# Keys turned by DVE and DMA instead of by PE in a lightning-attention and MoE layer

## The reference, cut to what matters

```python
qkv = jax.nn.silu(jnp.einsum('bnf,of->bno', x, w_qkv))
q, k, v = jnp.split(qkv, 3, axis=-1)
def step(kv, blk):
    qi, ki, vi = blk
    o_inter = jnp.einsum('bhmd,bhde->bhme', qi * q_decay, kv)
    qk = jnp.einsum('bhmd,bhnd->bhmn', qi, ki) * diag_decay
    o_intra = jnp.einsum('bhmn,bhne->bhme', qk, vi)
    kv_new = block_decay * kv + jnp.einsum('bhmd,bhme->bhde', ki * k_decay, vi)
    return (kv_new, o_inter + o_intra)
```

## Time and profile before

| | |
|---|---|
| time, median of 3 runs | 1790.89 us (1789.92 to 1792.35) |
| profiled execution | 1791.69 us, of which the profile's span is 1788.9 us |
| PE, DVE, ACT, POOL busy | 98%, 69%, 40%, 33% of the span |
| TensorE clock | granted 0.998 of full speed over the span |
| DMA | 249.37 MB, mean 139 GB/s |

### The profile page before, as it was taken

How to read it: one execution, slowest core, us unless ns; L and a number is a source line. 1 busy time by engine, 2 the same in 40 slices (tenths; PEclk the granted TensorE clock), 3 DMA queues, 4 the chain that set the end, 5 groups by cost and what they waited for, 6 DMA issues and landing times.

```text
span 1788.9 us, 34315 instructions
## 1 busy us (share of the span) xinstructions
PE 1751.8 (98%) x12213; PEld 1565.2 (87%) x12213; DVE 1228.4 (69%) x2463; ACT 709.8 (40%) x1331; POOL 585.8 (33%) x794
## 2 busy tenths in 40 slices
PE   6999999999999999999999999999999999999998
PEld 5888899999888888888888888889999999999997
DVE  7888777777566665666656666667777777766566
ACT  4333333343444444444444444443434343333332
POOL 2222254544434333433334333323232323200011
PEclk9999999999999999999999999999999999999999
DMA  6665431322367676676766766623222222210013
GB/s 216 220 222 210 139 110 62 108 86 83 106 196 225 199 220 204 205 215 201 215 210 203 218 201 207 210 71 95 63 83 71 72 72 71 74 46 1 1 60 106
DMA packets 194872, 249.37 MB, mean 139 GB/s; under 512 B 27280, under 2 KB 161936, under 8 KB 194704
## 3 DMA queue, kind: packets, MB, share of 16 engines
q1 hardware_dynamic: 150032, 138.09, 26.0%
q0 software_dynamic: 32256, 83.93, 14.4%
q10 hardware_dynamic: 12416, 25.17, 3.8%
HBM read 135.92 MB, written 111.17 MB: 138 GB/s over the span
## 4 chain that ended last, share of the span: by engine, by line
PE 93%; DVE 4%; issue 2%; ACT 1%; DMA 1%; SPq 0%; POOL 0%; DVEq 0%; ACTq 0%; POOLq 0%
PE bank L1166 7%; PE bank L1146 7%; PE bank L1168 7%; PE bank L1167 7%; PE bank L1148 7%; PE bank L1147 7%; PE bank L1190 6%; PE bank L1207 6%; PE bank L1198 6%; PE bank L1210 6%; PE bank L1230 5%; PE bank L1238 3%; PE bank L1219 3%; PE bank L1221 3%; PE bank L1220 3%; PE bank L1183 3%
## 5 line engine op out<-in xcount | busy, mean ns | idle before, releaser
L520 POOL DMA_DIRECT2D xsT<-rows_turned x384 | 209.9, 553 | 331.8 <-PE bank L1230 188.9
L1166 PE MATMUL bank<-wh,xh 128*128 128x256 f32 x1024 | 311.0, 304 | 0.0
L614 ACT ACTIVATE kv<-bank 128x512 f32<-128x512 f32 x256 | 152.9, 597 | 342.2 <-PE bank L1168 342.2
L1168 PE MATMUL bank<-wh,xl 128*128 128x256 f32 x1024 | 288.6, 282 | 0.0
L1167 PE MATMUL bank<-wl,xh 128*128 128x256 f32 x1024 | 288.2, 281 | 0.0
L529 POOL DMA_INDIRECT yk<-slot_y,pos x128 | 127.5, 996 | 278.1 <-DVE xr L930 229.8
L958 DVE SCALAR_TENSOR_TENSOR state<-state,hc,bank 128x128 f32<-128x128 f32 x448 | 155.8, 348 | 85.0 <-PE bank L1198 71.4
L1166 PEld LDWEIGHTS bank<-wh,xh 128*128 128x128 f32 x1024 | 193.8, 189 | 15.9 <-issue 15.9
L1146 PE MATMUL bank<-xh,wh 128*128 128x512 f32 x512 | 207.2, 405 | 0.0
L1148 PE MATMUL bank<-xh,wl 128*128 128x512 f32 x512 | 202.4, 395 | 0.0
L1147 PE MATMUL bank<-xl,wh 128*128 128x512 f32 x512 | 201.9, 394 | 0.0
(11 more groups left out here) (162 smaller groups left out, 3637.6 us busy)
## 6 DMA issues: line engine op xcount, KB each, us to landing
slot_x<-zeros ACTq DMA_DIRECT2D x8, 3072.0 KB, 9.9
we<-wexp_in SPq DMA_DIRECT2D x192, 128.0 KB, 2.4
xs<-slot_x SPq DMA_DIRECT2D x96, 256.0 KB, 3.7
rows_turned<-xz POOLq DMA_DIRECT2D x96, 256.0 KB, 2.8
xsT<-rows_turned POOLq DMA_DIRECT2D x384, 64.0 KB, 2.7
slot_y<-ys SPq DMA_DIRECT2D x96, 256.0 KB, 2.7
wd<-wdown_in SPq DMA_DIRECT2D x192, 64.0 KB, 2.5
raw<-wqkv_in SPq DMA_DIRECT2D x16, 384.0 KB, 4.0
```

The costliest lines, as they stand in the source:

```text
L520: pool.dma_start(xsT[q % 2][b * TB:(b + 1) * TB, :, :, :].rearrange("p a k j -> p a (k j)"), xz_back[q % 2, b]).then_inc(xsT_loaded[q % 2] ...
L614: act.activation(kv[i % 2][:, 2 * half:2 * half + 2, :].rearrange("p c n -> p (c n)"), bank[half][:], ACT.Silu).then_inc((k_silu, v_silu)[ ...
L1166: pe.matmul(dst, lh, rh, start=(k == 0), stop=False)
L1168: mm = pe.matmul(dst, ll, rh, start=False, stop=(k == KD - 1))
```

## The change

DVE turns the keys in blocks of 32x32 within their partitions, in one instruction (`kz`). SP stores them to DRAM (`keys_turned`), and after that has landed SP loads them in four DMAs, each of which moves the blocks of one group of 32 features to its partitions (`kT_by_group`). ACT then sets the blocks side by side (`kT`), one slot after the keys were made. PE's transposes and their bank use are gone; its scores move behind the first half of the output projection. DVE's `update_state` and `gated` move ahead of `decay_scores`. SP's program is written by slot, since it now has work in each: its older waits and DMAs are put to slots.

```diff
+            def store_keys(i):
+                sp.wait_ge(kz_ready, i + 1)
+                sp.dma_start(kz_dram[i % 2], kz[:].rearrange("p b c j -> p b (c j)")).then_inc(kz_stored, 16)
+
+            def load_keys(i):
+                sp.wait_ge(kz_stored, 16 * (i + 1))
+                sp.wait_ge(kT_ready, i)
+                for b in range(BLK):
+                    sp.dma_start(kT_by_group[b * TB:(b + 1) * TB, :, :, :].rearrange("p a c j -> p a (c j)"),
+                                 kz_back[i % 2, b]).then_inc(kT_loaded, 16)
...
+            for s in range(SLOTS + 1):
+                q0 = 2 * (s - EXPERT0)
+                experts = EXPERT0 <= s < EXPERT1
+                if EXPERT0 < s <= EXPERT1:
+                    pair_done(q0 - 1)
+                if s > FIRST_OUT + 3:
+                    store_last(s - FIRST_OUT - 4)
+                if s < NSTEP:
+                    store_keys(s)
+                if s in COMBINE:
+                    store_part(COMBINE.index(s))
+                if EXPERT0 - 1 <= s < EXPERT1:
+                    load_rows(q0 + 4)
+                if s < NSTEP:
+                    load_keys(s)
+                if 4 <= s < ROUTE0 + 3 * NSB and s % 3 == 1:
+                    load_rows_to_scatter(s // 3)
+                if s == EXPERT0 - 2:
+                    first_pairs()
+                if experts:
+                    pair_done(q0)
+                if EXPERT0 - 1 <= s < EXPERT1:
+                    load_rows(q0 + 5)
...
-            def copy_kT(i):
-                act.wait_ge(kT_mm, i + 1)
-                act.copy(kT[:], bank[2][:]).then_inc(kT_ready, 1)
+            def copy_kT(j):
+                act.wait_ge(kT_loaded, 16 * BLK * (j + 1))
+                act.wait_ge(s_mm, j)
+                act.copy(kT[:].rearrange("p c a j -> p a c j"), kT_by_group[:]).then_inc(kT_ready, 1)
...
+            def turn_keys(i):
+                dve.wait_ge(k_silu, i + 1)
+                dve.wait_ge(v_silu, i + 1)
+                dve.wait_ge(kz_stored, 16 * i)
+                dve.transpose(kz[:], kv[i % 2][:, :, 0:HD].rearrange("p c (b i) -> p b c i", i=TB)).then_inc(kz_ready, 1)
...
-            def turn_keys(i):
-                pe.wait_ge(sm_ready, i)
-                pe.wait_ge(mask_ready, NSB)
-                for c in range(CH):
-                    mm = pe.transpose(bank[2][:, ch[c]], kv[i % 2][:, c, 0:HD], ident[:])
-                mm.then_inc(kT_mm, 1)
```

More of the change, by code:

```diff
@@ L66, in lightning_moe @@
     xz_dram = nc.dram_tensor("rows_turned", [2, P, BLK, 4 * TB], F32, kind="Internal").ap()
+    kz_dram = nc.dram_tensor("keys_turned", [2, P, BLK, CH * TB], F32, kind="Internal").ap()
     part2 = nc.dram_tensor("part2", [T, D], F32, kind="Internal").ap()
@@ L252, in lightning_moe @@
         q_mm = sem("q_mm")
-        kT_mm = sem("kT_mm")
+        kz_ready = sem("kz_ready")
+        kz_stored = sem("kz_stored")
+        kT_loaded = sem("kT_loaded")
         g_mm = sem("g_mm")
@@ L385, in _, with load_rows_to_scatter @@
                 group(g)
[L387 to L391, removed]
+            def store_keys(i):
[7 more added lines that the diff above has]
+                                 kz_back[i % 2, b]).then_inc(kT_loaded, 16)
+            def load_rows_to_scatter(q):
                 for r in range(CH):
@@ L408, in load_experts, with first_pairs, pair_done @@
                     sp.dma_start(wd[r][j * F:(j + 1) * F, :], at(wdown, e)).then_inc(pair_loaded[r], 16)
[L410 to L429, removed]
+            def first_pairs():
+                sp.wait_ge(routed, 1)
+                sp.wait_ge(wgt_ready, 1)
+                for q in range(2):
+                    load_experts(q)
+                for r in range(CH):
+                    sp.wait_ge(scattered[r], 16 * TOPK * NT // CH)
+                for q in range(2):
+                    load_rows(q)
+            def pair_done(q):
+                sp.wait_ge(y_mm, q + 1)
+                if q + 2 < NPAIR:
+                    load_experts(q + 2)
+                sp.wait_ge(ys_ready, q + 1)
+                sp.dma_start(slot_y_pair[q], ys[q % 2][:]).then_inc(y_stored[q % 2], 16)
             def load_part(t):
@@ L433, in load_part, with store_part @@
                 sp.dma_start(xr[t % 2][:], part_tile[t]).then_inc(xr_loaded[t % 2], 16)
[L435 to L439, removed]
-                if s in COMBINE:
[L441 to L445, removed]
+            def store_part(t):
+                sp.wait_ge(summed, TOPK * (t + 1))
+                sp.dma_start(part2_tile[t], xr[t % 2][:]).then_inc(part2_stored[t % 2], 16)
@@ new lines, in load_last, with store_last @@
+            def load_last(b):
+                if b < 2:
+                    for r in range(2):
+                        sp.wait_ge(part2_stored[r], 16 * NT // 2)
+                else:
+                    sp.wait_ge(out_stored[b % 2], 16 * (b // 2))
+                sp.dma_start(res[b % 2][:], part2_grp[b]).then_inc(res_loaded[b % 2], 16)
+            def store_last(b):
+                sp.wait_ge(final, CH * (b + 1))
+                sp.dma_start(out_grp[b], res[b % 2][:]).then_inc(out_stored[b % 2], 16)
@@ new lines, in _ @@
+            sp.wait_ge(xn_stored, 16 * NSB)
+            next_head(1)
+            load_rows_to_scatter(0)
+            for s in range(SLOTS + 1):
[7 more added lines that the diff above has]
+                    store_keys(s)
+                if s in COMBINE:
+                    store_part(COMBINE.index(s))
[11 more added lines that the diff above has]
+                    load_rows(q0 + 5)
+                if s == EXPERT1:
+                    for r in range(2):
+                        sp.wait_ge(y_stored[r], 16 * NPAIR // 2)
+                    for t in range(2):
+                        load_part(t)
+                if s in COMBINE and COMBINE.index(s) + 2 < NT:
+                    load_part(COMBINE.index(s) + 2)
@@ L446, in _ @@
                 if s % NSB == 5 and s // NSB + 2 < NH:
                     next_head(s // NSB + 2)
[L449 to L458, removed]
+                if s == FIRST_OUT:
+                    for b in range(2):
+                        load_last(b)
@@ L1030, in _ @@
                     combine(COMBINE.index(s))
+                if s < 2:
+                    dve.wait_ge(tab_stored, 16)
+                if projects:
+                    turn_keys(s)
+                if attends:
+                    update_state(s - 1)
+                if experts:
+                    gated(q0)
                 if attends:
                     decay_scores(s - 1)
[L1033 to L1038, removed]
                 if projects:
@@ L1188, in scores @@
                 pe.wait_ge(kT_ready, j + 1)
+                pe.wait_ge(sm_ready, j)
+                pe.wait_ge(mask_ready, NSB)
                 for c in range(CH):
-                    mm = pe.matmul(bank[2][:, ch[c]], kT[:, ch[c]], qT[:, ch[c]], start=True, stop=True)
+                    mm = pe.matmul(bank[2][:, ch[c]], kT[:, c, :, :].rearrange("p a j -> p (a j)"), qT[:, ch[c]], start=True, stop=True)
                 mm.then_inc(s_mm, 1)
@@ L1276, in _ @@
                     project_kv(s, 0)
-                if attends:
-                    scores(s - 1)
+                    project_kv(s, 1)
                 if s > FIRST_OUT + 2:
                     turn_back(s - FIRST_OUT - 3)
[L1281 to L1284, removed]
                 if s == 0:
@@ L1290, in _ @@
                     keys_values(s - 1)
+                if experts:
+                    gate_up(q0)
                 if delivers:
                     project_out(s - 2, 0)
+                if attends:
+                    scores(s - 1)
                 if experts:
```

12 lines of the change are left out of this document (8 added, 4 removed).

## The result

The changed kernel takes 1848.9 us (median of 4, 1843.6 to 1852.1) against 1790.7: a ratio of 1.032, 95% interval 1.030 to 1.034. It is slower by 58 us, on the side that had 0.47, and outside my range of 1756 to 1820. The profiled execution, the fastest of the four, took 1843.6 us, its span 1841.8.

What follows compares the result with a forecast made beforehand. PE was taken to bound the kernel, with SP becoming the bound in expert slots: 1791.7 - 35.2 (PE) + 4 (DVE) + 6 (start) + 2 (slots 25, 26) + 20.2 (expert slots) = 1789 us, range 1756 to 1820.

Steps and rivals of the forecast that it cites:

- the side that had 0.47: Whole kernel: the chance given to the change making it slower, against 0.42 for faster and 0.11 for the same.
- PE's part: All 128 slots: dropping four transposes shortens PE by 0.44 us a slot, 0.11 each, 56 us in all.
- DVE's chain: Key turn, state steps and mask before PE's attend: fits with 0.15 us to spare; 4 us cost in all, 0 to 13.
- DVE did not become the bound: Rival: turn, state and mask late by 0.3 us each slot, PE waits before attend, 1809 us; chance 0.05.
- The start: Slot 1's scores: the first keys come late behind SP's row loads, so PE waits 6 us, 5 to 7.
- Slots 25 and 26: First experts' loads stand behind slot 25's key loads, and the key turn is queued behind: 2 us added, 0 to 6.
- The landing of the keys' store, in SP's round: Expert slots: SP waits for its store to land, taken as 3.0 us, before four loads; adds 20.2 us over 48 slots.
- 10.5 + 2.5 + 1.8 = 14.8 us: SP's round per expert slot: own work, landing less 0.5 us overlap, four issues; against 13.94 us for PE alone.
- the upper bound of the round: SP's round in expert slots: at most 16.2 us, with landing 3.7 and issues 2.5; lower bound 13.9.
- SP falls well behind: Rival, expert slots: landing 3.5, issues 0.5 and slowed transfers make SP's round 15.4 us, 1817 us; chance 0.18.
- SP keeps up: Rival, expert slots: landing 2.1 us, round 13.9, PE stays the bound and wins there too, 1747 us; chance 0.15.
- The Trainium skill's fit for a DMA: Keys' store landing: 2.0 us plus bytes at 436 GB/s, 2.6 us for 256 KB; round 14.4, end 1769 us.

Runs made afterwards that it cites:

- e4_store_first: The changed kernel with the keys' store issued ahead of the result store slot_y, not behind it; ratio 1.016 to the kernel before on the same chip.
- c_before: The kernel before, unchanged, run and traced again on a slow chip; 1889.5 us there, one run of 1890.9 us.
- e3_trip_alone: The kernel before, PE still turning the keys, plus DVE's turn and SP's store and loads that nobody reads; ratio 1.050 to the kernel before.
- e1_fill_wait: The changed kernel with the expert slots' four key loads issued after the slot's second pair is done; ratio 1.000 to the kernel before.

## Why the prediction was wrong

**PE's part held.** Without the transposes the step from the last gate matmul to the second of the next slot is 0.35 us, as said (timeline, PE, changed kernel; the earlier trace rows had 0.79):

```profile
1261.52 0.40 PE L1199 MATMUL bank<-xh,wl 128*128 128x512 f32 x1
1261.75 0.28 PE L1217 MATMUL bank<-wh,xh 128*128 128x256 f32 x1
1261.87 0.28 PE L1218 MATMUL bank<-wl,xh 128*128 128x256 f32 x1
```

Combining slots came to 10.55 (I had 10.5). As the earlier trace rows together say, the 0.27 us of a transpose's row is its length, and what its removal gives back is the distance of starts, 0.11.

**DVE's chain** had 4 us in my sum. Slots 2 to 24 came out 3.3 us and the combining slots 2.1 us longer than 0.44 less each, but PE's waits for the masked scores in them add up to about 1 us. Most of these slots won 0.43 us and the others about 0.3; what took the rest was not isolated. DVE did not become the bound.

**The start** cost 6.7 us in slot 1 (16.12 against 9.44), or 7.1 with the 0.44 that was due; I had 6. PE's wait for the keys is 5.4 us of it (L1236 above), inside the 5 to 7 forecast. The rest is a term that my sum does not have: the granted clock was half for 3.4 us behind that wait, which is 1.7 us of PE's work lost. ACT shows the late keys, and a window of the changed kernel the clock:

```profile
206.00 0.62 ACT L672 COPY kT<-kT_by_group 128x512 f32<-128x512 f32 x1 [4.91 <-DMA kT_by_group<-keys_turned]
...
206.50:210.00 3.50, 3.28 (x12) 3.02 (x13) 1.09 (x2) 0.12 (x1) 0.00 (x0) 0.51 0.26 75
```

**Slots 25 and 26** took 2.2 us more than before, and 3.1 more than before less 0.44 each (I had 2). PE waited 2.5 and 3.7 us there for the masked scores, which now stand on DVE behind `kz` and `state` too: in slot 25 DVE had waited 4.4 us for ACT's routing weights, in slot 26 6.0 us for the experts' rows (5.48 in the earlier trace rows). Before, PE waited 1.0 and 0.6 us for them.

**The landing of the keys' store, in SP's round, is the step that failed.** The mechanism is the one forecast: SP stops waiting for `down`, PE waits at `gate_up`, and the slot is SP's round. Of the sum "10.5 + 2.5 + 1.8 = 14.8 us" the first term held: the round of 15.9 us less the landing (3.9) and the four issues (2.0, I had 1.8) leaves 10.0, and I had 10.5 less the 0.5 that overlap. The landing of the keys' store, "I take 3.0", was 3.9. With 3.9 and 2.0 in their places the round is 15.9, the expert slots cost 72.0 us where I had 20.2, and 1789 becomes 1841, against 1843.6 measured in the profiled execution (the median of the four is 5 us more, and was not traced). The 3.7 of `xs`, which I named as the nearest row of a transfer behind `slot_y` and then left for a number nearer the stores, was the better row; even it was exceeded. Of the missing 0.9 us, e4_store_first gives 0.7 back by moving the store ahead of `slot_y`. The rest may be the traffic: with the DMA engines busy 0.73 of the time, not 0.69, `slot_y` and `rows_turned` also land 0.4 and 0.7 us later than before, though `xsT` does not (2.7 in both). That part was not isolated.

The range was also drawn too narrow for its own reasons: I wrote 16.2 us as the upper bound of the round, which gives 1856 us, and ended the range at 1820.

**The rivals.** The one that happened is "SP falls well behind" (0.18, 15.4 us, 1817 us), and it went 0.5 us a slot further. Its sum was off by itself: a landing of 3.5 and issues of 0.5 make 10.5 + 3.0 + 2.0 = 15.5 us before anything slows down, 1822 us. "SP keeps up" was ruled out by the landing. The Trainium skill's fit for a DMA (DMA: Bandwidth & Descriptors, "Anatomy of one DMA — SWDGE (gpsimd) path"), from which I had estimated 2.6 us for 256 KB, was short by a third for this store: the measured 3.9 us decides.

## What to carry to other kernels

When work is moved from a bound engine to a queue that has idle time, add up that queue's round: its own issues, the new issues, and each wait for a landing that stands in the middle. Here the landing wait cost its full length each time round, less what was issued meanwhile, and next to nothing once other issues stood between the store and the load that needs it: with that order, and the first store earlier, the trip went from 3.2% slower to 1.6% faster than the kernel before on chips where that takes 1791 us. And take the landing from a row that stands behind the same kind of neighbour on the same queue, not from one of the same size alone.

## What the runs showed of the hardware that was not expected

On three of the five chips the kernel before took 1885 to 1890 us against 1791, and 88 of the 100 us between the two traces are in the stage where POOL scatters rows (383.1 us against 295.4 for slots 0 to 26). In c_before PE stands for 61.8 us of it, against 4.3 on the first chip, and the granted clock is 0.91 in the mean, not 1.00, so that the same work keeps PE busy for 321.3 us, not 291.2. Kernels in which the scores wait for the trip from slot 0 on take 395 to 413 us for these slots on the slow chips, the others 383 to 392. e3_trip_alone, which makes the whole trip with nobody waiting for it on PE, takes 391.4, so the trip's traffic alone does not explain the longer ones. These are single executions on three chips. What stops the engines is open.

With the wait filled, 249 GB/s and a DMA share of 0.83 (e1_fill_wait) went with an expert slot of 14.2 us, where 222 GB/s at 0.73 came with one 1.7 us longer: the order of a queue mattered here, not the load.
